# Attention scores of a graph network: two heads' products of 64 rows against one product of 128 rows with zero blocks

## The reference, cut to what matters

```python
Q = (h @ Wq.T + bq).reshape(-1, H, DH)          # H = 4, DH = 64
K = (h @ Wk.T + bk).reshape(-1, H, DH)
V = (h @ Wv.T + bv).reshape(-1, H, DH)
scores = jnp.einsum('ehd,egd->ehg', Q[src], K[tgt]) / jnp.sqrt(jnp.float32(DH))
attn = jax.nn.softmax(scores, axis=-1)
msg = jnp.einsum('ehg,egd->ehd', attn, V[tgt]).reshape(-1, HID)
...
return jax.ops.segment_sum(proj, src, num_segments=n_nodes)
```

## Time and profile before

| | us |
|---|---|
| median of 3 runs | 5239.12 (5237.07 to 5248.7) |
| the profiled execution's own time | 5233.94 |
| its span | 5232.0 |
| attention over edges, three stretches | 769.6, 763.8 and 769.1 |
| TensorE, busy in the span | 3759.6 |
| GpSimd, busy in the span | 2424.9 |
| VectorE, busy in the span | 2729.3 |
| ScalarE, busy in the span | 1515.5 |

### The profile page before, as it was taken

The page is one execution under the profiler, slowest core; times in us unless marked ns, Lnnn a source line. Parts: engine busy times, 40 slices in busy tenths (PEclk is TensorE's granted clock), DMA queues, the critical chain, the costliest instruction groups (busy, mean ns, idle before and its releaser), DMA issues. The chain is left out here.

```text
span 5232.0 us, 112793 instructions
## 1 busy us (share of the span) xinstructions
PE 3759.6 (72%) x36105; PEld 2965.2 (57%) x36105; DVE 2729.3 (52%) x8902; ACT 1515.5 (29%) x6308; POOL 2424.9 (46%) x2373
## 2 busy tenths in 40 slices
PE   4666554888888788888887888888856455555677
PEld 3444332677777557777764777776645344444566
DVE  7666665556556545565554566565424233333423
ACT  1222220433334133333323333332222111121122
POOL 2666565455555145555523555553035444444201
PEclk9985556888788888888888788787867555555579
DMA  1110004455555145555523455553047222222100
GB/s 61 41 41 17 1 1 135 127 143 144 141 140 144 45 125 143 141 143 142 144 59 114 129 144 143 145 143 95 31 140 139 67 65 65 65 65 65 32 26 20
DMA packets 209041, 493.57 MB, mean 94 GB/s; under 512 B 73145, under 2 KB 97301, under 8 KB 207880
## 3 DMA queue, kind: packets, MB, share of 16 engines
q0 software_dynamic: 149120, 429.71, 29.7%
q1 hardware_dynamic: 59799, 62.33, 3.9%
HBM read 430.59 MB, written 62.94 MB: 94 GB/s over the span
## 5 line engine op out<-in xcount | busy, mean ns | idle before, releaser
L1144 POOL DMA_INDIRECT kv<-kv_table,ae_idx x1200 | 1232.4, 1027 | 1017.5 <-ACT ae_idx L1177 702.8
L1287 PE MATMUL sc_ps<-ae_q,ae_kT 64*128 64x64 f32 x9984 | 802.0, 312 | 97.3 <-issue 95.8
L1287 PEld LDWEIGHTS sc_ps<-ae_q,ae_kT 64*128 64x128 f32 x9984 | 741.6, 222 | 211.1 <-issue 202.2
L1221 DVE TENSOR_REDUCE ae_own<-sc_ps 128x64 f32<-128x1024 f32 x312 | 382.1, 1225 | 734.8 <-PE sc_ps L1287 502.2
L1300 PE MATMUL out_ps<-hid,kv 128*64 128x64 f32 x9984 | 529.3, 264 | 114.4 <-issue 90.2
L1904 POOL DMA_INDIRECT kv<-feature_table,pe_idx x412 | 411.1, 998 | 423.8 <-ACT pe_idx L1938 313.3
L741 POOL DMA_INDIRECT edge_records<-rec_c,idx x416 | 422.7, 1016 | 352.9 <-ACT rec_c L501 224.2
L1300 PEld LDWEIGHTS out_ps<-hid,kv 128*64 128x64 f32 x9984 | 449.7, 173 | 211.8 <-issue 189.6
L1154 ACT ACTIVATE ae_kT<-kT_ps 128x512 f32<-128x512 f32 x624 | 365.1, 595 | 665.3 <-PE kT_ps L1269 487.3
L1205 DVE TENSOR_TENSOR totals<-totals,out_ps 128x32 f32 x2496 | 447.1, 179 | 209.9 <-DVE totals L1205 4.1
L2033 PE MATMUL pe_out<-pe_wgt,kv 128*64 128x16 f32 x3328 | 298.9, 264 | 309.4 <-issue 224.4
(11 more groups left out here) (448 smaller groups left out, 5736.8 us busy)
## 6 DMA issues: line engine op xcount, KB each, us to landing
kv<-kv_table,ae_idx POOLq DMA_INDIRECT x1200
et_w<-in_EW SPq DMA_DIRECT2D x56, 192.5 KB
expert_in<-kv SPq DMA_DIRECT2D x14, 512.0 KB
et_xs<-expert_in SPq DMA_DIRECT2D x56, 128.0 KB, 3.8
expert_out<-et_o POOLq DMA_DIRECT2D x56, 128.0 KB, 3.6
edge_records<-rec_c,idx POOLq DMA_INDIRECT x416
kv<-feature_table,pe_idx POOLq DMA_INDIRECT x412
nodes_placed<-kv SPq DMA_DIRECT2D x12, 512.0 KB
```

Source lines behind the costliest of these rows:

```text
L1144: pool.indirect_dma_start(kv[:, k, u, :], None, kv_d, bass.IndirectOffsetOnAxis(ap=idx[:, k, u:u + 1], axis=0), bounds_check=last_row, oob ...
L1221: v.tensor_reduce(own[:, j, :, :].rearrange("p g x -> p (g x)"), sc_ps[:, j, :, :, :].rearrange("p e i (x w) -> p (e i x) w", w=W), axis=A ...
L1287: last = pe.matmul(sc_ps[:, k % 2, e, i, u * HW:(u + 1) * HW], kT[rows, u, i, :], q[rows, k % FEW, u, :, :].rearrange("p h w -> p (h w)"), ...
```

## The change

The queries go into `q` in two column blocks: block e = 0 holds them in rows 0 to 63 and block e = 1 in rows 64 to 127. The other half of each block is set to zero once at the start of a layer's attention, by VectorE. One product of all 128 rows with 128 moving columns then gives the scores of both key heads, since the zeros keep the heads apart. ScalarE's copies become copies of 64 rows, two for each one before. `sc_ps` is ordered by i, e in place of e, i, and the reduction and `sums` follow that order.

```diff
-        q = s("q", (P, FEW, BT, H, W))
+        q = s("q", (P, FEW, BT, 2, H, W))
...
                     for u in range(BT):
-                        act.activation(q[:, k % FEW, u, :, 0:WL], qT[:, :, bass.ds(rows[u], WL)], ACT.Copy).then_inc(m.q_ready, 1)
-                        act.activation(q[:, k % FEW, u, :, WL:W], qT[:, :, bass.ds(rows[BT + u], WH)], ACT.Copy).then_inc(m.q_ready, 1)
+                        for e in range(2):
+                            half = slice(e * DH, (e + 1) * DH)
+                            act.activation(q[half, k % FEW, u, e, :, 0:WL], qT[half, :, bass.ds(rows[u], WL)], ACT.Copy).then_inc(m.q_ready, 1)
+                            act.activation(q[half, k % FEW, u, e, :, WL:W], qT[half, :, bass.ds(rows[BT + u], WH)], ACT.Copy).then_inc(m.q_ready, 1)
...
+                for e in range(2):
+                    v.memset(q[(1 - e) * DH:(2 - e) * DH, :, :, e, :, :], 0.0).then_inc(m.q_clear, 1)
...
-                    for e in range(2):
-                        for i in range(2):
-                            pe.matmul(sc_ps[:, k % 2, e, i, :], ident_big[:, :], bc(marks[:, bass.ds(b * BT, BT), :], 2, H),
-                                      start=i == 0, stop=False)
-                    pe.wait_ge(m.q_ready, b * ROW + ROW)
+                    for i in range(2):
+                        for e in range(2):
+                            pe.matmul(sc_ps[:, k % 2, i, e, :], ident_big[:, :], bc(marks[:, bass.ds(b * BT, BT), :], 2, H),
+                                      start=e == 0, stop=False)
+                    pe.wait_ge(m.q_ready, b * (2 * ROW) + 2 * ROW)
...
                         for i in range(2):
-                            for e in range(2):
-                                rows = slice(e * DH, (e + 1) * DH)
-                                last = pe.matmul(sc_ps[:, k % 2, e, i, u * HW:(u + 1) * HW], kT[rows, u, i, :],
-                                                 q[rows, k % FEW, u, :, :].rearrange("p h w -> p (h w)"),
-                                                 start=False, stop=u == BT - 1 and i == 1)
+                            last = pe.matmul(sc_ps[:, k % 2, i, :, u * HW:(u + 1) * HW], kT[:, u, i, :],
+                                             q[:, k % FEW, u, :, :, :].rearrange("p e h w -> p e (h w)"),
+                                             start=False, stop=u == BT - 1)
...
                 transposes(0, 0, 0)
+                pe.wait_ge(m.q_clear, 2)
```

More of the change, by code:

```diff
@@ L1117, in attention_edges @@
         out_ps = pb(st, "out_ps", (P, 2, 512))
-        with phase(nc, "ae", "idx_ready", "turn", "q_ready", "sel_ready", "kT_ready", "kT_copied",
+        with phase(nc, "ae", "idx_ready", "turn", "q_clear", "q_ready", "sel_ready", "kT_ready", "kT_copied",
                    "scores_ready", "own_ready", "top_ready", "low_ready", "exp_ready", "z_ready", "rz_ready",
@@ L1125, in _ @@
                 wo, gam, bet, bo, ee, types, _, _ = update_parts(qT)
-                sp.wait_ge(m.q_ready, BATCHES * ROW)
+                sp.wait_ge(m.q_ready, BATCHES * 2 * ROW)
                 sp.dma_start(ee[:, :, :], t["Ee"][one].rearrange("a p h n -> p (a h) n")).then_inc(m.weights_loaded, 16)
@@ L1221, in step @@
                         v.tensor_reduce(own[:, j, :, :].rearrange("p g x -> p (g x)"),
-                                        sc_ps[:, j, :, :, :].rearrange("p e i (x w) -> p (e i x) w", w=W),
+                                        sc_ps[:, j, :, :, :].rearrange("p i e (x w) -> p (i e x) w", w=W),
                                         axis=AX.X, op=ALU.max).then_inc(m.own_ready, 1)
@@ L1298, in sums @@
                             for e in range(2):
-                                head, at = 2 * i + e, 2 * e + i
+                                head = 2 * i + e
                                 last = pe.matmul(o[e * DH:(e + 1) * DH, :], kv[:, k, u, D + head * DH:D + (head + 1) * DH],
-                                                 wgt[:, k % 2, u, at * H:(at + 1) * H, :].rearrange("p h w -> p (h w)"),
+                                                 wgt[:, k % 2, u, head * H:(head + 1) * H, :].rearrange("p h w -> p (h w)"),
                                                  start=i == 0, stop=i == 1)
```

## The result

The changed kernel takes 5203.71 us (median of 4 runs, 5195.38 to 5207.69), the kernel before 5241.56 beside it (4 runs, 5237.07 to 5248.7): ratio 0.9928, 95% interval 0.9907 to 0.995. It is faster, by 0.7%. The forecast was 5005 and its range began at 4850 and ended at 5185, so the result lies outside it, near the rival of no change. All of the gain is in the attention stretches: 2265.9 us against 2302.5.

What follows compares the result with a forecast made beforehand. The prediction took TensorE, by its clock and idle time in attention, as the bound. Its terms -94 - 108 - 35 + 3 = -234 us gave 5000, or 5005 us as a median; range 4850 to 5185.

Steps and rivals of the forecast that it cites:

- the rival of no change: Attention: TensorE's saving turns into idle time, or ScalarE's added copies come onto the path; 5230 to 5250 us, chance 0.06.
- So TensorE sets the pace, in two ways.: Attention: TensorE bounds the batch of 7.38 us, through its granted clock share of 0.80 and 1.07 us idle a batch.
- the ring: Theory after the result: four gathers' issue 4.90 us, sums' signal 1.1, index copy 0.20, next gather 0.99; 7.19 a turn.
- The steady rate of the scores: Score products: 16 full-height records take as long as 16 half-height pairs, 1.75 us at 2.4 GHz; counted as 0.
- The rival of exposed loads: Score products: load and stream don't overlap, 0.107 + 0.11 us a record; slower, 5680 us, chance 0.14.
- The crossings of shape: TensorE going between 128 and 64 rows around the scores: 0.3 us a batch saved, 94 us in all.
- The clock: TensorE in attention: half the time at 1.2 GHz goes, granted clock near 0.90 against 0.80, 108 us less.
- The idle time: TensorE's gaps in attention: 76 records a batch become 60; half of a possible 70 us taken, 35 us less.
- near 1.7: Sign in the changed profile: TensorE idle near 1.7 us a batch would mean the saving has turned into waiting.
- ScalarE: Query copies in attention: 8 more a batch, 0.96 us, covered by its wait for the transposes; counted as 0.
- The zeros: VectorE clearing 12 x 64 columns twice a layer: at most 6 us, counted as 3 us more.

Runs made afterwards that it cites:

- in the old form (136 us): Kernel before with only ScalarE's query copies split into two of 64 rows, products unchanged: 5367.29 us, ratio 1.0243, 136 us slower.
- with the ring gone (about 20 us on the other kind of chip): Changed kernel with half the gathers, or plain loads: 4083.8, 4081.86 us; kernel before with the same edits: 4060.53, 4062.55 (itself 4207.94).

## Why the prediction was wrong

**The step that failed** is the first: "So TensorE sets the pace, in two ways." It was drawn from TensorE's share of busy time and from a table of waits in which the others wait for it. In that table GpSimd waits 236.5 us for ScalarE's indices, and I read this as GpSimd waiting for TensorE. It is one side of a circle: TensorE's idle "issue" waits are the other, since they end when GpSimd stops issuing. I named the trickle of products 0.7 us apart and did not set it beside GpSimd's rows of the same microseconds. They lie in one timeline. The rival of no change said "the gaps come from somewhere that has its own pace"; it got a chance of 0.06 and is the one that the runs bear out, with 38 us left over that it had not given.

What the runs showed in its place: on the first kind of chip the ring sets the pace, with a median turn of 7.2 us in both kernels, above TensorE's 6.31 us of work a batch before and 5.39 after. With the gathers replaced, the old form does a batch in 5.04 us; with the index copy taken out of the ring, the turn falls to 6.95 and 6.85. Two things stay open: why the signal of the sums waits for the end of the gathers, and what of the gathers holds TensorE's products.

**The steady rate of the scores**: right. 16 records in 1.78 us at the full clock, against 1.75 forecast. By the rule that the prediction took from the Trainium skill, "TensorE: Matmul & The Clock Gate", section on packing small matmuls by row and column tiling, giving up the pairs would have cost some 0.9 us a batch; the trace does not agree, the scores are 0.15 us shorter. The rival of exposed loads (0.107 + 0.11 us a record) did not occur.

**The crossings of shape**: right in size, without effect on the time. 0.15 us went from the scores and 0.05 from the transposes, and marks to scores take 0.45 us from start to start against 0.54 in the old form (1398.85 to 1399.39 in the trace of before): 0.29 us, forecast 0.3. Of the 94 us counted for it, the end saw only what the ring lets through.

**The clock**: right in size, 0.80 to 0.91 against "near 0.90". Stretches at 1.2 GHz add up to 399 us in attention in place of 910, those longer than 9 us are 6 in place of 18. But 108 us were counted as if each microsecond of TensorE were one of the batch. The 6.69 us a batch at the full clock, on which they rest, was read too low: records were counted in stretches that begin and end inside dense work, and the 21 turns that touch these stretches last 7.12 us on average. The reason that I gave, that half-height products hold the clock down, is not shown: with plain loads the old form runs at 0.98. So the size of the clock's rise is no support for that reason.

**The idle time**: wrong in sign. A fall of 0.11 us a batch was forecast; it rose by 0.80. The text had named "near 1.7" as the mark of saving turned into waiting, and 1.87 is that.

**ScalarE**: 0.96 us more a batch was the forecast, and (1403.92 - 896.31) / 312 = 1.63 us of busy time came. The first copy's start to the last's grew by 1.9 us, because a change of half costs a step of 0.23 us. "I count 0" fails in the old form (136 us) and with the ring gone (about 20 us on the other kind of chip). The rival of no change had also named ScalarE's copies coming onto the path; in the old form they do. In the changed kernel, grouped copies that relieve ScalarE of 0.59 us a batch gain nothing measurable.

**The zeros and the rest**: nothing seen. Outside attention the spans are 5232.0 - 2302.5 = 2929.5 us before and 5201.2 - 2265.9 = 2935.3 after; this difference of 6 us was not followed up.

## What to carry to other kernels

An engine whose idle time ends with "issue" and whose products come at an even spacing is not the pace maker until the timeline of every other engine in the same microseconds has been laid beside it. Follow the buffer around: who issues the load, who frees the buffer, what signal releases the next load. If the sum of these steps equals the period, as 4.90 + 1.1 + 0.20 + 0.99 does, nothing outside them shortens it below that sum, and the cheapest gain is to take a step out, here the index copy. A change that relieves one engine by giving another more instructions should be priced with the new instructions alone as well, since the two effects can cancel.

## What the runs showed of the hardware

On one kind of chip, while GpSimd issues four indirect gathers in a row, TensorE runs on for the first two (busy for 0.97 or more of the first 2.5 us, over 279 turns of the changed kernel), then gets about one product in 0.7 us (busy for 0.15 to 0.21 of the time from 4.5 to 5.5 us), and is free from 6.0 us on, 1.1 us behind the last issue, with the DMA engines still 0.8 busy. Two gathers in a row do not hold its products. Its signal for the sums comes 1.1 us after the last of four gathers at the median, in the changed kernel 3.2 us after the last record's start and 4.0 at the 95th percentile. On the other kind, with the same program, neither is seen: the signal comes after 0.25 us at the median. With plain loads of the same bytes from SyncE's queue it comes after 0.25 us on both kinds, and no product is held. The same kernel takes a quarter longer on the first kind, 5238 against 4209 us. Not all of it is in attention: the changed kernel spends 2935 us outside it on the one and 2477 (4185.0 - 1708.2) on the other. Why the chips differ was not found.

Copies of ScalarE that change between the lower and the upper 64 rows start 0.23 us apart, those that stay on their rows 0.12 to 0.14.
